# Expert stage of a Mamba and mixture-of-experts layer: its six groups of four transposes per expert put together in three groups of eight

## What is computed

```
E = 32; K = 4; H = 1024; F = 512
CAP = 2 * (N * K // E)                      # 256 slots per expert
buf = zeros((E, CAP, H)).at[flat_e, slot].set(x_rep, mode='drop')
h  = silu(einsum('ech,ehf->ecf', buf, w1)) * einsum('ech,ehf->ecf', buf, w3)
ob = einsum('ecf,efh->ech', h, w2)
```

## Time and profile before

| | |
|---|---|
| median of 3 executions | 4121.24 us |
| lowest and highest of them | 4113.94 and 4123.34 us |
| the profiled execution's own time | 4121.58 us |
| its span, from the first to the last instruction | 4119.5 us |
| PE busy | 3812.2 us (93% of the span) |
| DVE busy | 3038.9 us (74%) |
| ACT busy | 2162.8 us (53%) |
| POOL busy | 1727.5 us (42%) |

### The profile page before, as it was taken

One profiled execution on the slowest core, in us unless ns is written; L12 is line 12 of the kernel. 1 busy time (PEld: TensorE's weight loads), 2 busy tenths in 40 slices (PEclk: granted clock), 3 DMA queues, 4 the chain that ended last, 5 costly groups with the idle time before them and its releaser, 6 DMA issues. The chain is left out here.

```text
span 4119.5 us, 59969 instructions
## 1 busy us (share of the span) xinstructions
PE 3812.2 (93%) x21088; PEld 3146.2 (76%) x21088; DVE 3038.9 (74%) x3711; ACT 2162.8 (53%) x2768; POOL 1727.5 (42%) x977
## 2 busy tenths in 40 slices
PE   8898588888888888799999989999999999999999
PEld 3444488788788788678888868888888888788887
DVE  7898799899999999887777745555555555455555
ACT  3688699899899899722222234444444444200000
POOL 0243299999999999823333310000000000122222
PEclk9999599999999999999999989999999999999999
DMA  6677843643643643355555556666776666677643
GB/s 232 243 293 258 306 135 116 174 138 115 178 139 115 182 135 117 131 197 183 185 194 187 209 182 234 239 239 238 241 243 236 231 232 232 226 279 267 201 162 118
DMA packets 328298, 819.60 MB, mean 199 GB/s; under 512 B 65920, under 2 KB 109696, under 8 KB 318784
## 3 DMA queue, kind: packets, MB, share of 16 engines
q1 hardware_dynamic: 296240, 750.13, 53.8%
q0 software_dynamic: 31744, 67.23, 5.5%
q10 hardware_dynamic: 144, 0.00, 0.0%
HBM read 603.38 MB, written 245.27 MB: 206 GB/s over the span
## 5 line engine op out<-in xcount | busy, mean ns | idle before, releaser
L1117 POOL TENSOR_TENSOR h<-h,c 128x1024 f32<-128x1024 f32 x512 | 1211.5, 2426 | 29.3 <-DVE h L1100 26.7
L1100 DVE TENSOR_TENSOR_SCAN h<-da,dbu 128x1024 f32<-128x1024 f32 x512 | 1135.0, 2272 | 49.0 <-ACT dbu L1062 21.0
L1149 PE MATMUL psy<-ident,h 128*128 128x128 f32 x4096 | 565.0, 282 | 94.1 <-POOL h L1117 74.5
L1070 ACT ACTIVATE da<-dl,ad 128x1024 f32<-128x1024 f32 x512 | 585.2, 1143 | 100.4 <-DVE h L1100 85.9
L1062 ACT ACTIVATE dbu<-psb 128x512 f32<-128x512 f32 x1020 | 548.8, 591 | 35.9 <-PE psb L1139 33.9
L1149 PEld LDWEIGHTS psy<-ident,h 128*128 128x128 f32 x4096 | 445.6, 142 | 147.9 <-POOL h L1117 111.8
L2054 DVE TENSOR_TENSOR wsp<-arena,wsp 128x2048 fp32r<-128x2048 f32 x198 | 447.7, 2289 | 101.4 <-ACT wsp L2006 101.4
L1892 POOL DMA_INDIRECT xg<-scratch_xn,ids x64 | 63.4, 991 | 1030.0 <-PE psT L1910 1008.7
L2006 ACT ACTIVATE wsp<-arena 128x2048 fp32r<-128x2048 f32 x198 | 370.7, 1910 | 30.4 <-DMA arena<-in_w 30.4
L1139 PE MATMUL psb<-m,du_taps 128*128 128x128 f32 x2048 | 294.9, 291 | 53.8 <-ACT dbu L1062 28.2
L1139 PEld LDWEIGHTS psb<-m,du_taps 128*128 128x128 f32 x2048 | 259.6, 194 | 87.1 <-ACT dbu L1062 65.9
(11 more groups left out here) (215 smaller groups left out, 7880.9 us busy)
## 6 DMA issues: line engine op xcount, KB each, us to landing
arena<-in_w SPq DMA_DIRECT2D x192, 1024.0 KB, 7.0
du_taps<-scratch_duT SPq DMA_DIRECT2D x496, 128.0 KB, 2.9
c<-scratch_c SPq DMA_DIRECT2D x64, 512.0 KB, 10.0
scratch_xT<-xT_s SPq DMA_DIRECT2D x32, 1024.0 KB, 4.9
scratch_ob<-ob SPq DMA_DIRECT2D x64, 512.0 KB, 2.7
xT_place<-scratch_xT SPq DMA_DIRECT2D x32, 1024.0 KB, 5.6
scratch_duT<-duT SPq DMA_DIRECT2D x52, 512.0 KB, 4.0
xz<-in_x SPq DMA_DIRECT2D x32, 512.0 KB, 5.6
```

Source lines behind the costliest of these rows:

```text
L1070: act.activation(da[k % 2][:, :], dl[:, i % 2, :], ACT.Exp, scale=ad[:, i % 2, n:n + 1]).then_inc(s_da, 1)
L1100: dve.tensor_tensor_scan(h[:, k % HR, :], da[k % 2][:, :], dbu[:, (k // GN) % 2, k % GN, :], 0.0, ALU.mult, ALU.add).then_inc(s_scan, 1)
L1117: pool.tensor_tensor(h[:, k % HR, :], h[:, k % HR, :], c[:, n, :], ALU.mult).then_inc(s_hc, 1)
L1149: mm = pe.matmul(psy[:, t, :], h[:, k % HR, t * P:(t + 1) * P], ident[:], is_transpose=True, start=(n == 0 and t % 4 == 0), stop=(n == NST ...
```

## The change

In the code that issues TensorE's instructions for an expert, three calls of `transpose_round` are moved ahead of the product that stood between them and the group before. Numbers of groups, banks, waits and the orders of ScalarE, VectorE, GpSimd and SyncE stay as they are.

```
                 gate_up(e, x, 1, 0)
                 gate_up(e, x, 1, 1, range(KH // 2))
                 round_of("h", 0, 0)
+                round_of("x", 0, 0)
                 gate_up(e, x, 1, 1, range(KH // 2, KH))
-                round_of("x", 0, 0)
                 pe.wait_ge(s_tlo, turn["h", 0, 0][0] + 1)
                 down(e, x, 0, 0)
                 round_of("h", 1, 0)
+                round_of("x", 0, 1)
                 down(e, x, 0, 1)
-                round_of("x", 0, 1)
                 pe.wait_ge(s_tlo, turn["h", 1, 0][0] + 1)
                 down(e, x, 1, 0)
                 round_of("x", 1, 0)
+                round_of("x", 1, 1)
                 down(e, x, 1, 1)
-                round_of("x", 1, 1)
```

## The result

Over 22 executions each, the changed kernel has a median of 4115.23 us (4107.02 to 4124.06) and the kernel before one of 4121.59 us (4112.66 to 4128.13). The ratio is 0.9985, with a 95% interval of 0.9979 to 0.9991: a gain of 6.4 us between the medians, of 3.7 to 8.7 us by the interval. The forecast was 4116.3 us, a gain of 5.3. The profiled execution took 4118.4 us, its span is 4116.5 us.

A forecast was written before the change was run, and what follows sets the result against it. TensorE's own instruction pace was taken to bound the expert stage. Three merged pairs save 0.17 us an expert, over 31 experts 5.3 us, with moved waits costed at nothing: 4121.58 us becomes 4116.3 us, range 4110 to 4123 us.

The forecast's parts named there:

- TensorE bounds the stage: Expert stage: TensorE busy 200.00 of 200 us at clock 1.00, waiting for nobody from expert to expert.
- A four costs 0.483 us, an eight 0.91 us: TensorE's stream: net cost of four transposes between matmuls, 0.483 us, and of eight in a row, 0.91 us.
- reading (a): An eight in the routing pass, 0.91 us against 0.97 for two fours: saves 0.17 us an expert, 5.3 us in all.
- 31 experts with three pairs each: Expert stage: 93 merged pairs, each saving 0.05 to 0.06 us; expert 31 has h groups alone and is unchanged.
- No gap for the waits inside a pair: Second group's waits inside each merged pair: priced between 0 and 0.105 us a pair, taken as 0.
- Rival 1: Waits inside a merged pair start the second group 0.06 us or more late; 4121 to 4126 us, chance 0.17.
- Moved instructions cost nothing: Each x group moves up past twelve matmuls, 2.7 us; its waits and the gathers were costed at nothing.
- The slack of x(0,1): Second pair, behind h(1): the rest of x(0,0) ends about 2912.2, x(0,1) starts at 2913.43; slack 1.2 us.
- rivals 2 and 3: TensorE waits mid-pair for a bank, 4156 us, chance 0.03; clock falls after an eight, 4184 us, chance 0.02.
- rival 4: More than the sum: matmuls behind a break recover sooner, or measurement scatter; 0.1 us a pair, 4112 us, chance 0.13.

The follow-up runs named there:

- The groups of the identity: Kernel before plus four or eight unread identity transposes an expert between gate and up products: periods 36.023 and 36.450 us, against 35.540.
- The splits: Kernel before, five groups split into twos around three or six matmuls: 35.560, 35.982 us an expert; with eight extra unread transposes as two fours around three matmuls: 36.467.

## Why the prediction was right

- **TensorE bounds the stage.** Right: no wait repeats from expert to expert, before or after, and TensorE is busy throughout at a granted clock of 1.00. One detail was misread: between the waits of 10.3, 4.9 and 2.2 us lies one of 2.3 us, at the entry of the pass behind the stage.
- **A four costs 0.483 us, an eight 0.91 us.** Right. The groups of the identity measured 0.483 and 0.910, and the periods 0.170 us an expert against a forecast of 0.17. The exactness has some luck in it: reading (a) rests on a single eight, and in the changed kernel single eights, read the same way, cost 0.89 or 0.93 us, in equal numbers. Only their mean is 0.91.
- **31 experts with three pairs each, all worth the same.** Right: 0.056 to 0.057 us each, by the kernels with one pair.
- **No gap for the waits inside a pair.** Right. This was the term for which no row at full clock existed, with bounds of 0 and 0.105 us. The starts of the two fours are 0.43 to 0.44 us apart. Rival 1 is refuted.
- **Moved instructions cost nothing.** Right. The slack of x(0,1) was put a little too low. The rest of x(0,0) starts right behind the product of tile 1 now, since ScalarE's part is through earlier:

```profile
2841.71 0.68 DVE L2049 TENSOR_TENSOR xT_place<-psT,xT_place 128x512 fp32r<-128x512 f32 x1
```

  In this timeline of the changed kernel it ends at 2842.39, and x(0,1) starts at 2843.99 (above): 1.6 us instead of 1.2. The rest that x(1,1) needs ends at 2848.74 in the same expert and x(1,1) starts at 2850.33, a slack of 1.6 us where 1.5 were expected.
- **What the saved 0.056 us is.** Here the words went further than the rows. I called it a part "that is paid once a group, whatever its length", and "belongs to the break". The splits show that it is not a price for every break: with three matmuls between, a further break costs 0.004 us (0.020 for five) to 0.017 us (0.927 less 0.910). The larger part is a slow stretch of the matmuls behind a run of transposes, which a close break cuts short. Nor does it go by breaks alone. In the starts of experts 5 to 28, the nine intervals from the second to the eleventh matmul behind a group hold on average 0.036 us more than undisturbed ones behind a four, and 0.025 behind an eight. Of the 0.057 us that a pair saves, 2 x 0.036 - 0.025 = 0.046 are there, and only 0.010 are saved at once. The sum came out right because (a) counts the matmuls behind a group, and because twelve or more of them stood behind each group it was read from, as they do in the changed kernel.
- **The absolute time.** 4116.3 against 4115.23 us is closer than the method can claim. The sum starts from a single execution, 4121.58 us, which happened to lie on the median of the 22 (4121.59), while single ones lie up to 9 us from it. What the prediction can take credit for is the difference of 0.170 us an expert.
- **The prices of rivals 2 and 3.** Their times, 4156 and 4184 us, add the loss to the kernel before and leave out the gain of 5.3 us that both would have kept; by the prediction's own terms they are 4150 and 4178. Nothing else hangs on them.
- **Faster by more than the sum (rival 4).** The interval of the ratio allows 3.7 to 8.7 us. The periods put 5.3 us on the change, and no run shows a pair that saved more than 0.057 us. The 1.1 us between that and the difference of the medians lie within the interval; the traces give no other source for them.

## What to carry to other kernels

When small operations are gathered into longer runs, first split the cost of a run into what each operation takes and what the change of work takes, by comparing a short and a long run in the same trace. Here nine tenths belonged to the transposes themselves, so halving the breaks could bring no more than 0.06 us a pair. And before joining, read what the work between the groups was covering: the pair costs nothing only as long as the readers of the first bank are through in time, and one swapped instruction on another engine turned a gain of 0.17 us an expert into a loss of 2.4, or of 2.2 in the experts that kept the full clock. A sum that comes out right to a hundredth can still name the wrong cause for its last term; runs that split that term are what tells.

## What the runs showed of the hardware that I had not expected

The slow stretch behind a run of transposes appears even where no other engine reads the group, and it is shorter behind an eight (0.025 us) than behind a four (0.036). What causes it stays open; no run takes it apart. A wait of 2.14 us in the middle of a pair lowered the granted clock in three experts of thirty, while 3.66 us of transposes without a matmul never did. And with 32 transposes in a row, the first gate matmul of some experts starts late with nothing in the trace that it waited for. The waits of that kernel's TensorE between 2400 and 3800 us have it as a row of its own:

```profile
PE psG L1920 <- issue: 2.1, 5, 0.6
```

Five times in the stage, 2.1 us in all by this row. The real price is higher: the second of the two experts above is 0.42 us longer because of it, the expert behind a late start is 0.1 to 0.2 us longer too, and over the twenty experts, with four late starts, the sum is 3.0 us. The code loops over four experts at a time, and the late ones are four apart. With sixteen in a row no such row appears.
